# Query and key parts stored once and repeated by the loads, and the values' bias added by VectorE, in a four-layer network on one Trainium2 core

## The chip, the core and the metric

The kernel runs on one core of a Trainium2 chip (trn2). The core has TensorE (PE in the profile, with PEld for its weight loads), VectorE (DVE), ScalarE (ACT), GpSimd (POOL), SyncE (SP, which here only issues DMA transfers), and 16 DMA engines that move data between HBM and the on-chip memories. The metric is the device time of one execution in microseconds, the median over runs. Lower is better.

## The reference

A residual network of four layers on `x` of shape 8 x 512 x 128. Every layer adds an attention and a feed-forward of the same normalised input. The three attentions that the change touches, with 16 heads of 8 numbers each:

```python
# layer 0: causal, with alibi                     (8 batches, 512 tokens)
qkv = x @ w_qkv.T + b_qkv;  q, k, v = heads(qkv)
scores = q @ k.T / sqrt(8) - (distance), masked;  out = softmax(scores) @ v
return out @ w_out.T + b_out
# layer 2: causal, relative positions
scores = (Q @ K.T + Q @ pek[idx].T) / sqrt(8), masked;  attn = softmax(scores)
out = attn @ V + attn @ pev[idx];  return out @ Wo.T
# layer 3: no mask; queries, keys and values are one projection
q = x @ wq.T + bq;  out = softmax(q @ q.T / sqrt(128)) @ q;  return out @ wu.T + bu
```

Layer 1 is a linear attention, which the change leaves alone. The feed-forwards are two blockwise fp4 layers, a local attention network, and a routed mixture of 8 experts.

## The kernel before

The stages run one after the other, each in a `Scope` that ends with a barrier of all engines. Scores are products of bf16 numbers that together keep fp32 accuracy: every query and every key is split into three bf16 parts of 8 rows each (first, second, third), and a product over 48 rows sums six pairings of parts. So the contraction needs the query parts in the order 1,2,3,1,2,1 (`QROWS`) and the key parts in the order 1,1,1,2,2,3 (`KROWS`).

**The projection**, `split_projection` (L725), runs for each attention before it, over 8 batches of 512 tokens. A job is one projection of one batch: TensorE makes `h_ps` (L750), ScalarE writes `FULL` and the first part (L769, L773), VectorE makes the other two parts (L783, L785, L787), and SyncE and GpSimd store the parts to DRAM (`query_rows_d`, `key_rows_d`), six stores of 128 KB per job: part 1 three times, part 2 twice, part 3 once, so that the DRAM copy has all 48 rows. Even ones are issued by SyncE (L797), odd ones by GpSimd (L818); in layer 3, where GpSimd scatters rows for the experts, SyncE issues all 12 of a job. `PARTS` is a ring of four; ScalarE waits for the stores of job i-4 before it writes it again. Layers 0 and 2 have two jobs per batch (queries, keys) and also the values: four 128x128 products of the batch with the weights, each followed by a one-row product that adds the bias (L756, L757), and a copy by ScalarE (L776). The DRAM rows are read only after the projection's barrier.

**The causal and the last attention**, `turned_attention` (L826), is written out step by step for t from -14 to the end, 32 steps per batch. Two groups of heads live in SBUF rows 0 to 47 and 64 to 111 of `QS` and `KS`. SyncE loads two batches ahead (L922, L925): four transfers of 48 rows, 384 KB each, in pieces of 1 KB in layer 0 and 512 B in layer 3 (there keys go to `KN`, and GpSimd regroups them). In the order of SyncE's queue, the loads of batch b+2 come at step 33 of batch b (keys of layer 3 at step 20). Behind them in the same queue stand, for each quad T of heads (8 steps), four small transfers of the row maxima, `a_soft_QS<-a_soft_MT` (L964, L966), two rows each, issued at step 8T-5. TensorE waits for them at step 8T before the turned scores (L1064). At the start come loads of batch 0, four `alibi_d` transfers of 4 rows x 16 pieces of 1 KB in layer 0 (L941), and loads of batch 1.

**The relative attention**, `relative_heads` (L277), goes in quads of four heads, 32 quads. At the start of each quad SyncE issues the loads of the next one (L361): 48 rows of 4 KB for the queries and 48 for the keys, 192 KB each. For each head it then issues the band load, the skew store, two bias loads and two band stores. TensorE first needs the next quad's operands four scores later, in `relative` (L497). SyncE's queue is in order: an instruction that waits holds all behind it.

The profile drops the layer's digit from names: `a_proj_PARTS` is the tile of `a0_proj`, `a2_proj` or `a3_proj`.

## Time and profile before

| | us |
|---|---|
| median of 3 runs (4264.11 to 4271.95) | 4265.2 |
| the profiled execution | 4260.68 |
| its span in the trace | 4258.7 |
| projection of layer 0, first product to last ScalarE copy | 63.7 to 111.6 |
| causal attention, first product | 151.9 |
| projection of layer 2 | 2359.2 to 2416.1 |
| relative attention, first product | 2432.2 |
| projection of layer 3, first product | 3555.3 |
| last attention, first product | 3817.6 |

The rest are the feed-forwards, the linear attention, norms and set-up. The mean granted TensorE clock of the profiled execution was 0.783 of full speed. The profile's page gives totals; what a change in one stage does is read from the timeline of that stage, engine by engine: the start of an instruction, its length, and in brackets how long its engine sat idle before it and what released it.

### The profile page before, as it was taken

What the parts mean: (1) busy time and instruction counts of PE and PEld (TensorE: products, weight loads), DVE (VectorE), ACT (ScalarE), POOL (GpSimd) and SP (SyncE); (2) the same over time, 40 slices, a digit from 0 to 9 for tenths busy, and PEclk for the clock granted to TensorE, in tenths of its full rate; (3) what the DMA queues carried; (4) which work ended last, traced back from release to release, by engine and by line L of the source; (5) the groups of instructions that cost most, each with busy time, mean ns of one, the idle gap of its engine ahead of it and who ended that gap; (6) DMA issues with size and microseconds to landing.
All of it is one profiled execution on the core that took longest, in us unless ns stands there. A gap on an engine that the chain in (4) does not pass through costs nothing. (4 is left out here: it accounts for less than half of the span.)

```text
span 4258.7 us, 67695 instructions
## 1 busy us (share of the span) xinstructions
PE 2931.0 (69%) x21547; PEld 1596.1 (37%) x21547; DVE 2349.2 (55%) x4792; ACT 1746.5 (41%) x4244; POOL 826.7 (19%) x1061
## 2 busy tenths in 40 slices
PE   5588846374635787777776687777778722768885
PEld 2344424253423444444443343333333311762221
DVE  4556467454855566666663354444445453138885
ACT  2355511211213455455553244444444401227775
POOL 2100001021113444444441300000000004112220
PEclk9789867686767999999998666666666655889998
DMA  3432110000001000000000577777777615663331
GB/s 113 79 56 52 38 53 0 8 1 6 1 14 48 10 19 18 18 10 18 18 18 3 170 189 196 187 192 192 187 193 192 161 42 158 174 146 55 66 61 37
DMA packets 462309, 340.77 MB, mean 80 GB/s; under 512 B 64351, under 2 KB 424986, under 8 KB 461986
## 3 DMA queue, kind: packets, MB, share of 16 engines
q1 hardware_dynamic: 441474, 308.78, 29.4%
q0 software_dynamic: 8704, 20.99, 1.8%
q10 hardware_dynamic: 11808, 7.08, 0.6%
q8 instruction: 155, 2.54, 0.3%
q14 instruction: 168, 1.38, 0.1%
HBM read 174.71 MB, written 146.81 MB: 75 GB/s over the span
## 5 line engine op out<-in xcount | busy, mean ns | idle before, releaser
L1158 DVE TENSOR_REDUCE a_soft_NM<-a_soft_s_ps 128x2 f32<-128x1024 f32 (+3 forms) x512 | 514.2, 1021 | 204.3 <-PE a_soft_s_ps L1093 132.8
L1192 ACT ACTIVATE a_soft_PTS<-a_soft_st_ps 128x512 f32<-128x512 f32 (+3 forms) x1024 | 458.3, 521 | 147.9 <-PE a_soft_st_ps L1069 101.7
L465 PE MATMUL a_soft_pt_ps<-net_ident,a_soft_PR 128*128 128x128 f32 x1280 | 330.1, 370 | 123.2 <-ACT a_soft_PTS L567 115.8
L613 ACT ACTIVATE a_soft_PR<-a_soft_s_ps,a_soft_least 128x128 f32<-128x128 f32 (+3 forms) x512 | 263.9, 527 | 338.7 <-DVE a_soft_least L588 241.8
L1064 PE MATMUL a_soft_st_ps<-a_soft_QS,a_soft_KS 50*128 50x512 bf16 (+4 forms) x1024 | 257.8, 359 | 60.1 <-ACT a_soft_PTS L1192 32.2
L465 PEld LDWEIGHTS a_soft_pt_ps<-net_ident,a_soft_PR 128*128 128x128 f32 x1280 | 184.1, 181 | 220.8 <-ACT a_soft_PR L613 160.0
L1106 PE MATMUL a_soft_o_ps<-a_soft_PTS,a_soft_VR 128*32 128x512 f32 (+3 forms) x2048 | 240.9, 544 | 0.1
L2275 PE MATMUL f_run_ps<-f_run_WQKV,f_run_HT 128*128 128x512 f32 x384 | 228.9, 687 | 15.2 <-DVE f_run_RS L1496 8.0
L2608 ACT ACTIVATE f_run_PB<-f_run_ps,f_run_MX 128x128 f32<-128x128 f32 x512 | 180.3, 378 | 134.0 <-DVE f_run_MX L2490 134.0
L2413 POOL TENSOR_TENSOR f_run_QK<-f_run_QK,f_run_T 128x512 f32<-128x512 f32 x128 | 163.4, 1277 | 365.6 <-DVE f_run_T L2468 363.2
L569 DVE COPY a_soft_PTS<-a_soft_pt_ps 128x512 f32<-128x512 f32 (+3 forms) x320 | 169.5, 530 | 72.6 <-PE a_soft_pt_ps L465 40.0
L588 DVE CUSTOM_DVE_ANT_0 a_soft_s_ps<-a_soft_s_ps,a_soft_BIAS 128x128 f32<-128x128 f32 (+1 forms) x256 | 92.9, 363 | 205.1 <-PE a_soft_s_ps L510 177.4
L583 DVE TENSOR_REDUCE a_soft_far_least<-a_soft_s_ps 128x1 f32<-128x128 f32 (+1 forms) x256 | 91.2, 356 | 192.8 <-PE a_soft_s_ps L510 191.5
L510 PE MATMUL a_soft_s_ps<-a_soft_KS,a_soft_QS 48*128 48x128 bf16 (+3 forms) x512 | 194.5, 380 | 1.1 <-ACT a_soft_PR L613 0.9
L2252 PE MATMUL f_run_ps<-net_ident,f_run_PB 128*128 128x128 f32 x512 | 88.2, 330 | 154.5 <-DVE f_run_PB L2478 154.5
L439 POOL COPY a_soft_VR<-net_XN 128x128 f32 (+1 forms) x32 | 9.4, 296 | 918.3 <-PE a_soft_o_ps L486 918.1
L2490 DVE TENSOR_REDUCE f_run_MX<-f_run_ps 128x8 f32<-128x1024 f32 x64 | 78.4, 1225 | 188.3 <-PE f_run_ps L2242 188.3
L567 ACT ACTIVATE a_soft_PTS<-a_soft_pt_ps 128x512 f32<-128x512 f32 (+3 forms) x320 | 149.1, 466 | 74.9 <-PE a_soft_pt_ps L465 67.2
L2421 POOL TENSOR_TENSOR f_run_QK<-f_run_QK,f_run_RN 128x512 f32<-128x512 f32 x128 | 169.0, 1320 | 31.3 <-issue 18.2
L1064 PEld LDWEIGHTS a_soft_st_ps<-a_soft_QS,a_soft_KS 54*128 54x128 bf16 (+1 forms) x1024 | 72.0, 94 | 264.0 <-ACT a_soft_PTS L1192 182.1
L1088 PE MATMUL a_soft_s_ps<-a_soft_QS,a_soft_KS 48*128 48x512 bf16 x512 | 118.4, 397 | 53.3 <-DMA a_soft_QS<-query_rows_d 27.6
L2252 PEld LDWEIGHTS f_run_ps<-net_ident,f_run_PB 128*128 128x128 f32 x512 | 70.8, 166 | 198.3 <-issue 198.3
(382 smaller groups left out, 6395.5 us busy)
## 6 DMA issues: line engine op xcount, KB each, us to landing
a_soft_BIAS<-skew_d SPq DMA_DIRECT2D x256, 191.0 KB, 4.3
band_d<-a_soft_PR SPq DMA_DIRECT2D x256, 191.0 KB, 3.8
skew_d<-a_soft_RS SPq DMA_DIRECT2D x128, 256.0 KB, 4.5
a_soft_PB<-band_d SPq DMA_DIRECT2D x128, 256.0 KB, 3.1
f_run_W<-in_L_ffn_w SPq DMA_DIRECT2D x72, 256.0 KB, 2.7
query_rows_d<-a_proj_PARTS SPq DMA_DIRECT2D x96, 128.0 KB, 3.4
key_rows_d<-a_proj_PARTS SPq DMA_DIRECT2D x96, 128.0 KB, 3.8
a_soft_QS<-query_rows_d SPq DMA_DIRECT2D x32, 384.0 KB
```

The costliest lines, as they stand in the source:

```text
L465: last = pe.transpose(pt_ps[:, slot, kb * P:(kb + 1) * P], PR[:, n % NPR, OFF + kb * P:OFF + (kb + 1) * P], ident[:])
L510: pe.matmul(s_ps[:, n % 4, 0:w], q_blk(sl, h, j), KS[:, sl, h * S:h * S + w], start=True, stop=True).then_inc(scores_ready, 1)
L569: eng.tensor_copy(dst, src).then_inc(pt_copied[0], 1)
L613: act.activation(PR[:, n % NPR, OFF:OFF + width(j)], s_ps[:, n % 4, 0:width(j)], ACT.Exp, bias=least[:, n:n + 1], scale=-1.0).then_inc(pro ...
L1064: last = pe.matmul(st_ps[:, e % 3, q0:S], cols(KS, KX, buf, par, g, kb * P, P), cols(QS, KX, buf, par, g, q0, S - q0), start=True, stop=fu ...
L1106: last = pe.matmul(o_ps[32 * h:32 * h + 32, q0:S], VR[:, T % 2, h, kb, :], PTS[:, T % 2, h, kb, q0:S], start=(kb == 0), stop=(kb == TB - 1 ...
L1158: dve.tensor_reduce(NM[:, T % 2, j, p, :], s_ps[:, ring["s", a] % 2, :, 0:width(j)], AX.X, ALU.max, negate=True).then_inc(max_ready, 1)
L1192: act.activation(PTS[:, T % 2, 2 * p + par, kb, q0:S], st_ps[:, e % 3, q0:S], ACT.Exp, scale=scale).then_inc(probs_ready, 1)
L2275: pe.matmul(out, HT[:, j * P:(j + 1) * P], WQKV[:, v // B, i * LINNER:(i + 1) * LINNER], start=True, stop=True).then_inc(m["q_ready"], 1)
L2413: pool.tensor_tensor(QK[:, j, i, :], QK[:, j, i, :], T2[:, i, :], ALU.add).then_inc(m["added"], 1)
L2421: pool.tensor_tensor(heads(QK[:, j, i, :]), heads(QK[:, j, i, :]), bcast(RN[:, j, i, :], 64), ALU.mult).then_inc(m["qk_scaled"], 1)
L2608: last = act.activation(PB[:, j % 2, h, :], ps[:, where["s", v, j] + h // 4, (h % 4) * P:(h % 4 + 1) * P], ACT.Exp, bias=MX[:, j % 2, h:h ...
```

## The change

- In three attentions the projection stores every part once (`PART_ROWS`): three stores of 128 KB per job, two by SyncE and one by GpSimd; in layer 3 three by SyncE per batch. The DRAM tensors have 24 rows. Layer 3 keeps one tensor, and both its queries and keys are read from it.
- Each load of 48 rows becomes three (`PAIRS`): rows 0 to 23, 24 to 39 and 40 to 47 of the SBUF tile. For queries they read parts 1-3, 1-2 and 1. For keys they read part 1 three times, part 2 twice and part 3 once, by a source whose outermost dimension has step 0 and size 3 or 2. Bytes per load stay the same. `turned_attention` has 12 load transfers per batch for 4, `relative_heads` 6 per quad for 2.
- The values' bias is loaded once into all 128 partitions (`shift`), the one-row products are gone, and VectorE's addition (after the batch's last job) replaces ScalarE's copy.
- The small stages that filled the row of ones are gone.

```diff
-    NDMA = 2
+    NDMA = 6
...
                 for t, src in ((QS, qd3), (KS, kd3)):
-                    sp.dma_start(t[:, sl, :], src[ds(b, 1), :, u * 4 * S:(u + 1) * 4 * S].rearrange("a p f -> (a p) f")).then_inc(opnd_loaded[sl], 16)
+                    for n, (at, m) in enumerate(PAIRS):
+                        of = src[ds(b, 1), :, u * 4 * S:(u + 1) * 4 * S].rearrange("a p f -> (a p) f")
+                        rows = t[at * HD:(at + m) * HD, sl, :]
+                        if src is qd3:
+                            sp.dma_start(rows, of[0:m * HD, :]).then_inc(opnd_loaded[sl], 16)
+                        else:
+                            of = of[n * HD:(n + 1) * HD, :]
+                            sp.dma_start(rows, bass.AP(of.tensor, of.offset, [[0, m]] + [list(d) for d in of.ap])).then_inc(opnd_loaded[sl], 16)
...
-QROWS = ((0, 0), (8, 1), (16, 2), (24, 0), (32, 1), (40, 0))
-KROWS = ((0, 0), (8, 0), (16, 0), (24, 1), (32, 1), (40, 2))
+PART_ROWS = ((0, 0), (8, 1), (16, 2))
+PAIRS = ((0, 3), (3, 2), (5, 1))
...
-                        pe.matmul(out, XNT[:, b * S + j * P:b * S + (j + 1) * P], values[0], start=True, stop=False)
-                        last = pe.matmul(out, values[2], values[1], start=False, stop=True)
+                        last = pe.matmul(v_ps[:, b % 2, j * P:(j + 1) * P], XNT[:, b * S + j * P:b * S + (j + 1) * P], values[0],
+                                         start=True, stop=True)
...
-                if values is not None:
-                    act.wait_ge(v_ready, b + 1)
-                    act.activation(values[3][:, 4 * b:4 * b + 4, :, :].rearrange("p a h (j d) -> p (a h) j d", d=HD),
-                                   v_ps[:, b % 2, :].rearrange("p (j h d) -> p h j d", j=TB, d=HD), ACT.Copy).then_inc(v_copied, 1)
...
+                if values is not None and i % NJ == NJ - 1:
+                    b = i // NJ
+                    dve.wait_ge(v_ready, b + 1)
+                    shift = bass.AP(values[1].tensor, values[1].offset, [list(values[1].ap[0]), [HD, H], [0, TB], [1, HD]])
+                    dve.tensor_tensor(values[2][:, 4 * b:4 * b + 4, :, :].rearrange("p a h (j d) -> p (a h) j d", d=HD),
+                                      v_ps[:, b % 2, :].rearrange("p (j h d) -> p h j d", j=TB, d=HD), shift, ALU.add).then_inc(v_copied, 1)
...
-            def load(b, t, d, sem):
+            def load(b, t, d, queries, sem):
                 for par in range(2):
-                    dst = t[64 * par:64 * par + KR6, b % 2, :]
...
+                    for n, (at, m) in enumerate(PAIRS):
+                        dst = t[64 * par + at * HD:64 * par + (at + m) * HD, b % 2, :]
+                        of = d[b, 0:m * HD] if queries else d[b, n * HD:(n + 1) * HD]
...
+                        if not queries:
+                            of = bass.AP(of.tensor, of.offset, [[0, m]] + [list(x) for x in of.ap])
+                        sp.dma_start(dst, of).then_inc(sem, 16)
```

SyncE's queue in the relative attention at the start of a quad, before: operands of the next quad (L361), band load, skew store, bias loads, band stores.

```order
L361 DMA a_soft_QS<-query_rows_d 48x2048
L361 DMA a_soft_KS<-key_rows_d 48x2048
L394 ISA
L395 DMA a_soft_PB<-band_d 128x4x128
L365 REGISTER_ALU
L368 DMA skew_d<-a_soft_RS 128x4x128
```

The same place in the changed kernel, where the query loads are L365, the key loads L368 and the band load L402.

```order
L365 DMA a_soft_QS<-query_rows_d 24x2048
L365 DMA a_soft_QS<-query_rows_d 16x2048
L365 DMA a_soft_QS<-query_rows_d 8x2048
L368 DMA a_soft_KS<-key_rows_d 24x1x2048
L368 ISA
L368 DMA a_soft_KS<-key_rows_d 16x1x2048
L368 ISA
L368 DMA a_soft_KS<-key_rows_d 8x2048
L398 REGISTER_ALU
L401 ISA
L402 DMA a_soft_PB<-band_d 128x4x128
```

Four more transfers stand ahead of the band load and of all that follows it.

SyncE's queue in the causal attention, the loads of batch b+2 and what is next behind them, before:

```order
L966 DMA a_soft_QS<-a_soft_MT 2x512 x4
L925 DMA a_soft_KS<-key_rows_d 48x8x512 x2
L925 DMA a_soft_QS<-query_rows_d 48x8x512 x2
L980 DMA heads_d<-a_soft_OS 9x512 x4
L966 DMA a_soft_QS<-a_soft_MT 2x512 x4
```

And in the changed kernel the loads of that place alone (now L938):

```order
L938 DMA a_soft_KS<-key_rows_d 24x8x512
L938 DMA a_soft_KS<-key_rows_d 16x8x512
L938 DMA a_soft_KS<-key_rows_d 8x8x512
L938 DMA a_soft_KS<-key_rows_d 24x8x512
L938 DMA a_soft_KS<-key_rows_d 16x8x512
L938 DMA a_soft_KS<-key_rows_d 8x8x512
L938 DMA a_soft_QS<-query_rows_d 24x8x512
L938 DMA a_soft_QS<-query_rows_d 16x8x512
L938 DMA a_soft_QS<-query_rows_d 8x8x512
L938 DMA a_soft_QS<-query_rows_d 24x8x512
L938 DMA a_soft_QS<-query_rows_d 16x8x512
L938 DMA a_soft_QS<-query_rows_d 8x8x512
```

The head stores and the row maxima (now L993 and L979) come eight transfers later in the queue.

VectorE's row in the projection of layers 0 and 2, changed kernel: the addition of the values stands behind every second job.

```order
L785 TENSOR_TENSOR a_proj_REST<-a_proj_FULL,a_proj_PARTS 128x512
L787 CAST a_proj_PARTS<-a_proj_REST 128x512
L789 TENSOR_TENSOR a_proj_PARTS<-a_proj_REST,a_proj_PARTS 128x512
L794 TENSOR_TENSOR a_vall<-a_proj_v_ps,a_shift 128x512
L785 TENSOR_TENSOR a_proj_REST<-a_proj_FULL,a_proj_PARTS 128x512
```

VectorE has seven instructions per batch where it had six, and ScalarE four where it had five.

## Rows read from the trace of the kernel before

**Rows 1.** Page, part 1: each engine's busy time, share of span, instructions.
```profile
PE 2931.0 (69%) x21547; PEld 1596.1 (37%) x21547; DVE 2349.2 (55%) x4792; ACT 1746.5 (41%) x4244; POOL 826.7 (19%) x1061
```

**Rows 2.** Timeline, SyncE queue, causal attention: start us, length, line, transfers.
```profile
203.62 1.33 SPq L925 DMA_DIRECT2D a_soft_KS<-key_rows_d  x2
204.99 1.28 SPq L925 DMA_DIRECT2D a_soft_QS<-query_rows_d  x2
...
210.43 2.54 SPq L966 DMA_DIRECT2D a_soft_QS<-a_soft_MT  x4
217.01 0.62 SPq L987 DMA_DIRECT2D a_soft_SC<-heads_d  x1
```

**Rows 3.** Timeline, TensorE, same place; idle before and releaser in brackets.
```profile
217.60 0.43 PE L1064 MATMUL a_soft_st_ps<-a_soft_QS,a_soft_KS 54*128 54x512 bf16 x2 [3.60 <-DMA a_soft_QS<-a_soft_MT]
```

**Rows 4.** Windows: engines' busy times, TensorE clock, DMA share, GB/s.
```profile
132.00:142.00 10.00, 0.00 (x0) 0.00 (x0) 0.00 (x0) 0.00 (x0) 0.68 (x3) 0.50 1.14 162
154.00:155.00 1.00, 0.73 (x12) 0.40 (x8) 1.00 (x2) 0.00 (x0) 0.00 (x0) 0.50 0.27 87
155.00:156.00 1.00, 0.38 (x7) 0.14 (x4) 1.00 (x2) 0.00 (x0) 0.00 (x0) 0.50 0.33 99
```

**Rows 5.** DMA view, window 153 to 157 us: packets by size.
```profile
DMA packets 276, 0.28 MB, mean 70 GB/s; under 512 B 19, under 2 KB 275, under 8 KB 275
```

**Rows 6.** Timeline, SyncE, start of the causal attention.
```profile
130.47 1.34 SPq L925 DMA_DIRECT2D a_soft_KS<-key_rows_d  x2
...
134.25 0.70 SPq L941 DMA_DIRECT2D a_soft_KS<-alibi_d  x2
```

**Rows 7.** Timeline, TensorE, first product of the causal attention.
```profile
151.89 0.30 PE L1088 MATMUL a_soft_s_ps<-a_soft_KS,a_soft_QS 52*128 52x128 bf16 x2 [40.93 <-DMA a_soft_KS<-alibi_d]
```

**Rows 8.** Timeline, SyncE, relative attention, one group's load.
```profile
2707.76 0.48 SPq L361 DMA_DIRECT2D a_soft_QS<-query_rows_d  x1
2708.34 1.01 SPq L361 DMA_DIRECT2D a_soft_KS<-key_rows_d  x1
2711.24 0.39 SPq L395 DMA_DIRECT2D a_soft_PB<-band_d  x1
```

**Rows 9.** Timeline, TensorE, relative attention, same group.
```profile
2713.18 0.60 PE L497 MATMUL a_soft_r_ps<-a_rel_k,a_soft_QS 48*128 48x128 bf16 x4 [1.66 <-DMA a_soft_KS<-key_rows_d]
```

**Rows 10.** Waits, 2600 to 3200 us: engine, line, releaser, us, times, longest.
```profile
PE a_soft_r_ps L497 <- DMA a_soft_KS<-key_rows_d: 32.9, 15, 3.1
```

**Rows 11.** Timeline, SyncE, last attention, a key load in the loop.
```profile
3869.46 1.33 SPq L922 DMA_DIRECT2D a_soft_KN<-key_rows_d  x2
...
3878.03 2.73 SPq L964 DMA_DIRECT2D a_soft_QS<-a_soft_MT  x4
```

**Rows 12.** Timeline, TensorE, last attention, first product and first turned product.
```profile
3817.60 1.03 PE L1088 MATMUL a_soft_s_ps<-a_soft_QS,a_soft_KS 48*128 48x512 bf16 x4 [27.57 <-DMA a_soft_QS<-query_rows_d]
...
3835.11 0.61 PE L1064 MATMUL a_soft_st_ps<-a_soft_QS,a_soft_KS 50*128 50x512 bf16 x2 [1.21 <-DMA a_soft_QS<-a_soft_MT]
```

**Rows 13.** Tile a_proj_v_ps: ns min/median/max, first and last start.
```profile
L776 ACT ACTIVATE a_vall<-a_proj_v_ps x8: 597/597/601, 70.8 to 111.0; 128x512 f32<-128x512 f32 x8
L776 ACT ACTIVATE net_XN<-a_proj_v_ps x8: 597/597/598, 2368.5 to 2415.5; 128x512 f32<-128x512 f32 x8
```

**Rows 14.** Timeline, TensorE, values of one batch, third projection.
```profile
2381.36 0.48 PE L757 MATMUL a_proj_v_ps<-a_rows 1*128 1x128 f32 x2
2381.77 1.99 PE L750 MATMUL a_proj_h_ps<-net_XNT,a_W 128*128 128x512 f32 x2
```

**Rows 15.** Timeline, VectorE, same projection, one job to the next.
```profile
2384.92 0.69 DVE L783 TENSOR_TENSOR a_proj_REST<-a_proj_FULL,a_proj_PARTS 128x512 f32<-128x512 f32 x1 [2.83 <-ACT a_proj_PARTS L773]
...
2386.79 0.69 DVE L783 TENSOR_TENSOR a_proj_REST<-a_proj_FULL,a_proj_PARTS 128x512 f32<-128x512 f32 x1
```

**Rows 16.** Timeline, SyncE, end of the causal attention's projection.
```profile
113.43 2.94 SPq L797 DMA_DIRECT2D key_rows_d<-a_proj_PARTS  x3
```

**Rows 17.** Timeline, TensorE, first product after the last layer's projection.
```profile
3647.46 1.12 PE L2050 MATMUL f_run_xt_ps<-net_ident,f_run_ROWS 128*128 128x128 f32 x4 [82.36 <-DMA f_run_ROWS<-expert_rows_d]
```

66 lines of the change are left out of this document (29 added, 37 removed).

## The prediction

> **What bounds the kernel now.** I read the page first: TensorE is busy 2931.0 us, 69% of the span [rows 1], so no engine is full over the whole, and each of the three attentions must be read in its own timeline. In the causal attention I followed SyncE through one load of the operands. Four transfers are issued from 203.62 to 206.3, the row maxima (`MT`) of the next quad from 210.43 to 213.0 [rows 2], and TensorE then sits idle for 3.60 us until 217.60, released by those maxima [rows 3]. The store of the heads' results issued in between is as late: SyncE's next instruction, which waits for it, starts at 217.01 [rows 2]. So what is queued behind a load lands behind it, and a load here lies on the path already. At the start, TensorE's first product waits until 151.89 for the alibi rows [rows 7], which are issued at 134.25 behind the loads of batch 0 [rows 6]. In the relative attention the loads are issued at 2707.76 and 2708.34 [rows 8], TensorE waits for them 1.66 us until 2713.18 [rows 9], and it does so in 15 of some 20 quads, 32.9 us in 600 [rows 10]. In the last attention the first product waits for operands until 3817.60 and the first turned product for maxima until 3835.11 [rows 12]. The projections of layers 0 and 2 take 5.74 and 6.71 us per batch (7 periods from 70.8 to 111.0 and from 2368.5 to 2415.5) [rows 13], and there TensorE goes from one batch to the next without a gap. The projection of layer 3 ends when GpSimd has scattered the experts' rows: TensorE waits 82.36 us [rows 17].
>
> **How a transfer is spread, and what a piece costs.** This decides the case. While all 16 DMA engines work on loads into 48 rows, they move 162 GB/s (132 to 142 us), 10.1 GB/s or 101 ns per KB each. From 154 to 156 us the share falls to 0.27 and 0.33, that is 4 to 5 of 16 engines, with 87 and 99 GB/s [rows 4]. The stretch 153 to 157 has 276 packets, 19 of them small [rows 5], so 257 of 1 KB: the 4 x 64 pieces of the four alibi transfers, whose outermost dimension is 4. They were spread over four engines though each had 64 pieces to share, and these four engines end later than the rest by exactly that work. Alone, they moved about 22 GB/s each, 47 ns per KB. I conclude that an engine's share is cut from the outermost dimension. The new key loads have an outermost source dimension of 3 and 2 (24 and 16 rows in SBUF), and a common cut of both sides gives 3 and 2 engines; the query loads are cut in 12, 16 and 8. No row shows such a repeated source, and if the cut follows the SBUF rows it would be 12 and 16 engines; both are kept. The Trainium skill, "DMA: Bandwidth & Descriptors", section "Why a DMA increments its semaphore by 16 and not by 1", says that a transfer runs on the largest number of engines up to 16 that divides the slowest dimensions of both sides, lowest-numbered first, and its rules for kernel authors warn of a leading zero-stride broadcast. The alibi rows agree. By it the sum is the one below; without it, rival A.
>
> The first engine's work for one batch of `turned_attention` is then, for each of the two head groups, keys 64 + 64 + 8 KB and queries 16 + 8 + 8 KB, together 336 KB against 96 KB before. The row maxima, two rows, use the same first engines.
>
> **Causal attention, six loads in the loop.** Before: 96 KB at 101 ns, 10 us, seen as 205.3 to 215.3, and maxima 2.3 us later. After: 336 KB at 47 ns is 15.8 us; the queries' part (64 KB) is shared with many engines and may go at 60 to 100 ns, so 17 to 19 us, and I take 17.5. SyncE's eight more issues at 0.65 us each (1.33 for two [rows 2]) end before that and cost nothing. The next maxima land 7.5 us later, and nothing covers it, since TensorE waits for them now: 6 x 7.5 = 45 us. Bounds per load: 5 us (47 ns throughout) and 25 us (101 ns throughout: 34 us for 10). **Its start:** loads of batch 0 end 7.5 us later, but alibi pieces behind them, now contended, go faster: +3.5; the first maxima wait for batch 1's load: +4.5. Together 8 (3 to 42).
>
> **Relative attention, 31 loads.** The first engine has 84 KB per quad (21 pieces of 4 KB) for 24. At 47 ns per KB it is 3.9 us against 2.4 at the contended rate: +1.5. Four more issues at 0.5 us each, from the rows' 0.48 and 1.01 [rows 8], put the last key transfers 2 us later, partly beside that: together +3, between +1 (issue and data overlap) and +8 (84 KB at 101 ns plus issue). SyncE then waited until 2711.24 for the band's stores, so it is not itself held up. TensorE waits already, and its next loads are tied to the same quad's end, so the delay recurs: 31 x 3 = 93 us (31 to 250).
>
> **Last attention.** Keys alone are 272 KB on the first engine, in 512 B pieces. At 47 to 54 ns per KB that is 13 to 14.7 us against 4.9. Start: keys +9, then the queries, so the first product +9; first maxima behind batch 1's load, +4. In the loop keys are issued at 3869.46 and the maxima at 3878.03 [rows 11]; keys end at 3871.3 + 14 = 3885.3, the maxima about 2.3 later at 3887.6, where 3880.8 + 2.3 = 3883.1 was enough: +4 each, x 6 = 24. The query loads (128 KB for 96) end before their maxima are issued: 0. Together 37 (15 to 145).
>
> **Gains.** One-row products: a pair starts at 2381.36 and the next product at 2381.77 [rows 14], 0.41 us, four per batch, 1.66 us. VectorE's two jobs take 2 x 1.87 (2384.92 to 2386.79 [rows 15]) and the addition, of the size of its 0.69 us subtraction, 0.7: 4.45 us. Layer 2: 6.71 becomes 5.05, TensorE still last, 8 x 1.66 = 13. Layer 0: 5.74 - 1.66 is 4.1, so VectorE's 4.45 is last in the fast half: 8 to 12, I take 10. ScalarE loses a copy that nothing waited for. Stores: layer 0's last six are issued until 116.37, the last three taking 2.94 us [rows 16], and four of a batch's instead of six on SyncE end some 2 us sooner, in both layers 1.5 to 2. A stage less in layer 2, 1. Layer 3: the scatter is last anyway, 0, unless its wait of 82 us were the stores'. Sum -28 (-20 to -34).
>
> **The sum.** The profiled execution took 4260.7 us, 4.5 under the median of the three. 4260.7 + 8 + 45 + 93 + 37 - 28 = 4415.7. I take 4415.
>
> **Rivals.** A: the cut follows the SBUF rows, so all or 12 engines share. The first engine's rows are 8 for 6 in a relative quad and 128 KB for 96 in a batch of the others: +3 us x 6, +5 at the starts, and in the relative attention issue alone, +1 to +2 x 31; 18 + 5 + 46 - 28 = +41, 4302. For it: no row has a repeated source. Against it: the alibi transfers. B, the side of faster: the loads land no later than now, because a repeated row comes cheaper and the issue overlaps; then only the gains stay, 4233. The point is 0.9 us more per relative quad (28 / 31). For it: the loads of the relative attention run beside other traffic; against it: TensorE waits for them in three of four quads. C: few engines are no faster than many on these rows, 101 ns per KB: 6 x 25 + 42 + 250 + 145 - 28 = +559, 4820. Against it: rows 4, on four engines. Between forecast and C lies a part of it, as where a longer wait also lowers the granted TensorE clock in the relative attention.
>
> **How the numbers follow.** Forecast 0.69, A 0.14, B 0.08, C 0.09. A measurement of this kernel tells 0.2%, 8.5 us, from no change. Faster is B with 0.08, within 0.2% is the low edge of A, 0.03, slower the rest, 0.89. The forecast's own range is 4330 to 4540 (low and middle bounds); to hold 8 in 10 it reaches into A and a little towards C: 4290 to 4570.
>
> **What would show it.** In the profile after: at each load of the causal attention TensorE idles about 11 us on `MT` (3.60 now) with a DMA share near 0.2; the wait of L497's successor is 4 to 5 us per quad; the key loads' landings grow most; projections run at 5.05 and about 4.5 to 5 us per batch. If the DMA share stays at one in the loads, the step on spreading is wrong and A holds; if it falls but landings take 35 us, C.

## The result, and the profile after

The changed kernel takes 4440.0 us (median, 4433.5 to 4446.9), the kernel before 4268.6 beside it: a ratio of 1.039, 95% interval 1.0375 to 1.0405. It is slower by 171 us; 4415 was forecast, with 4290 to 4570 as the range. The profiled executions, 4433.53 and 4260.68 us, differ by 172.9.

The spans of the two traces, cut at the same events, give this account. The right column is what the same stage was forecast to add.

| stage | before, us | after, us | difference | forecast |
|---|---|---|---|---|
| set-up, to the first product of layer 0's projection | 63.6 | 65.5 | +1.9 | 0 |
| projection of layer 0 with its drain | 56.9 | 42.2 | -14.7 | -12 |
| causal attention, start | 44.8 | 56.9 | +12.1 | +8 |
| causal attention, first to last turned product | 358.6 | 424.1 | +65.5 | +45 |
| middle layers and the set-up of layer 2 | 1835.3 | 1850.8 | +15.5 | -1 |
| projection of layer 2, to the first relative product | 73.0 | 51.0 | -22.0 | -15 |
| relative attention, first to last product | 970.7 | 1030.6 | +59.9 | +93 |
| to the first product of the last attention | 414.7 | 422.9 | +8.2 | +9 |
| last attention, to the first turned product | 17.5 | 22.0 | +4.4 | +4 |
| last attention, turned products | 382.2 | 423.5 | +41.3 | +24 |
| the end | 41.4 | 42.2 | +0.8 | 0 |

The sum is near and the large signs are as forecast, but three terms are off by 17 to 33 us, and the middle, where -1 was forecast, lost 15.5.

SyncE's queue in the causal attention of the changed kernel (timeline: start us, length, line, transfers), where [rows 2] stood:

```profile
199.90 2.43 SPq L979 DMA_DIRECT2D a_soft_QS<-a_soft_MT  x4
202.71 10.54 SPq L938 DMA_DIRECT2D a_soft_KS<-key_rows_d  x6
213.30 6.15 SPq L938 DMA_DIRECT2D a_soft_QS<-query_rows_d  x6
219.50 1.53 SPq L993 DMA_DIRECT2D heads_d<-a_soft_OS  x4
221.07 2.52 SPq L979 DMA_DIRECT2D a_soft_QS<-a_soft_MT  x4
```

And TensorE at that place (timeline; in brackets the idle time before and its releaser), for [rows 3]:

```profile
228.02 0.62 PE L1077 MATMUL a_soft_st_ps<-a_soft_QS,a_soft_KS 54*128 54x512 bf16 x2 [14.93 <-DMA a_soft_QS<-a_soft_MT]
```

Read the two together. The wait on the maxima grew from 3.60 to 14.93 us. The maxima are issued at 221.07, 21.2 us after the previous ones, where it was 9.6 (200.81 to 210.43). From their issue to TensorE's product it is 6.95 us now and was 7.17. By the semaphore events of both traces, maxima of a quad without a load land 3.4 to 3.6 us after their issue, and those behind a load 5.8 to 7.4. So the maxima wait behind the load on the DMA engines in both kernels alike, some 3 us, and what has grown is that they are issued late. SyncE spends 16.7 us in issuing twelve transfers.

The six transfers of the keys take 1.76 us each as a mean, where one of 48 rows took 0.67, but they are not alike. Here are the first (24 rows, outermost dimension 3) and the last (8 rows, outermost dimension 8):

```profile
202.71 0.80 SPq L938 DMA_DIRECT2D a_soft_KS<-key_rows_d  x1
209.91 3.34 SPq L938 DMA_DIRECT2D a_soft_KS<-key_rows_d  x1
```

The second took 0.70 and the fifth 3.28. So it is not its own shape that makes an issue long, but what has been issued in front of it. The kernel before shows the same where loads pile up: at the start of its causal attention the last of eight operand loads, of 48 rows, is held too.

```profile
141.52 3.07 SPq L925 DMA_DIRECT2D a_soft_QS<-query_rows_d  x1
```

While SyncE issues the keys the DMA engines are far from busy (windows: TensorE, its weight loads, VectorE, ScalarE, GpSimd, granted clock, DMA share, GB/s):

```profile
204.00:209.00 5.00, 4.54 (x68) 2.50 (x66) 3.57 (x6) 4.18 (x10) 0.29 (x1) 1.00 0.22 54
209.00:214.00 5.00, 3.95 (x64) 2.07 (x60) 3.30 (x4) 2.52 (x9) 0.00 (x0) 1.00 0.18 61
...
222.00:226.00 4.00, 0.00 (x0) 0.00 (x0) 0.00 (x0) 0.00 (x0) 0.00 (x0) 0.50 0.13 42
```

A share of 0.18 to 0.22 is three to four engines of sixteen while the keys are issued; [rows 4] had 1.14 in such a load. In between, with the queries, it rises to 0.73. At the end it is two engines at 20 GB/s each.

In the relative attention TensorE waits for the operands 71.0 us in 18 quads of a stretch of 600 us (waits, 2690 to 3290 us: engine, line, releaser, us, times, longest), where [rows 10] had 32.9 in 15:

```profile
PE a_soft_r_ps L504 <- DMA a_soft_KS<-key_rows_d: 71.0, 18, 6.3
```

One such quad, SyncE and then TensorE, for [rows 8] and [rows 9]:

```profile
2784.09 2.44 SPq L365 DMA_DIRECT2D a_soft_QS<-query_rows_d  x3
2786.62 2.26 SPq L368 DMA_DIRECT2D a_soft_KS<-key_rows_d  x3
2789.12 0.41 SPq L402 DMA_DIRECT2D a_soft_PB<-band_d  x1
```

```profile
2792.74 0.60 PE L504 MATMUL a_soft_r_ps<-a_rel_k,a_soft_QS 48*128 48x128 bf16 x4 [3.96 <-DMA a_soft_KS<-key_rows_d]
```

In the last attention a key load in the loop, for [rows 11], is held at the issue too: 12.88 us for six transfers, so the maxima follow 17.9 us after the previous ones instead of 11.6.

```profile
3997.35 2.64 SPq L977 DMA_DIRECT2D a_soft_QS<-a_soft_MT  x4
4000.04 12.88 SPq L938 DMA_DIRECT2D a_soft_KN<-query_rows_d  x6
4012.96 2.27 SPq L990 DMA_DIRECT2D heads_d<-a_soft_OS  x4
4015.27 2.70 SPq L977 DMA_DIRECT2D a_soft_QS<-a_soft_MT  x4
```

The term that was not seen stands in the set-up of layer 2. SyncE's queue there in the changed kernel:

```profile
2394.73 1.45 SPq L137 DMA_DIRECT2D a_shift<-in_L_attn_pev  x1
2396.23 10.33 SPq L137 DMA_DIRECT2D a_far_key<-in_L_attn_pek  x16
2420.04 0.35 SPq L255 DMA_DIRECT2D a_turn_ring<-in_L_attn_Wq  x1
```

and in the kernel before:

```profile
2331.00 0.58 SPq L137 DMA_DIRECT2D a_rows<-in_L_attn_pev  x1
2331.63 5.54 SPq L137 DMA_DIRECT2D a_far_key<-in_L_attn_pek  x16
2339.57 0.35 SPq L255 DMA_DIRECT2D a_turn_ring<-in_L_attn_Wq  x1
```

From the bias load to the next stage it is 25.3 us, and was 8.6. The windows of the changed kernel show nothing at work in it but DMA at 4 GB/s:

```profile
2396.00:2406.00 10.00, 0.00 (x0) 0.00 (x0) 0.00 (x0) 0.00 (x0) 0.00 (x0) 0.50 0.05 4
2406.00:2416.00 10.00, 0.00 (x0) 0.00 (x0) 0.00 (x0) 0.00 (x0) 0.00 (x0) 0.50 0.07 4
```

The projections gained more than forecast. VectorE's addition in the two of them (ns min/median/max, first and last start), for [rows 13]:

```profile
L794 DVE TENSOR_TENSOR a_vall<-a_proj_v_ps,a_shift x8: 682/684/686, 72.7 to 103.0; 128x512 f32<-128x512 f32 x8
L794 DVE TENSOR_TENSOR net_XN<-a_proj_v_ps,a_shift x8: 682/684/686, 2446.5 to 2477.1; 128x512 f32<-128x512 f32 x8
```

Seven periods are 4.33 us each in layer 0 and 4.37 in layer 2. What TensorE does meanwhile in layer 2 is in the windows of the kernel before,

```profile
2380.00:2390.00 10.00, 10.00 (x32) 5.56 (x31) 5.48 (x10) 3.56 (x7) 5.69 (x11) 0.77 0.74 220
2390.00:2400.00 10.00, 10.00 (x30) 5.35 (x28) 5.19 (x9) 5.22 (x9) 3.78 (x8) 0.72 0.86 261
```

and of the changed one:

```profile
2450.00:2456.00 6.00, 4.87 (x21) 2.60 (x20) 5.63 (x10) 3.23 (x6) 1.39 (x4) 1.00 0.62 182
2456.00:2462.00 6.00, 4.39 (x22) 2.85 (x23) 5.56 (x11) 3.21 (x6) 1.39 (x3) 1.00 0.64 188
```

Before, TensorE was busy without a gap at a granted clock of 0.72 to 0.77. Now it is busy 73 to 81% of the time at 1.00, the level of 2.4 GHz, and VectorE is busy 93 to 94%. The projection of layer 2 that was TensorE's is VectorE's. In layer 0 the clock was not always low before: from 90 to 110 us TensorE was busy without a gap at 1.00.

```profile
90.00:110.00 20.00, 20.00 (x80) 12.35 (x80) 12.77 (x22) 12.10 (x20) 11.68 (x23) 1.00 0.90 275
```

So these windows show which clock each projection had, and not what sets it.

### The profile page after: what moved, and what is told of

The parts are those of the page before. It is cut to its first block and busy times, and to the rows that moved or that the text cites. A ratio compares the mean times of both kernels' runs of the same rounds, so it can differ in the third digit from the quotient of the medians.

```text
span 4431.7 us, 67657 instructions
## 1 busy us (share of the span) xinstructions
PE 2883.7 (65%) x21419; PEld 1559.6 (35%) x21419; DVE 2359.1 (53%) x4806; ACT 1738.0 (39%) x4228; POOL 791.3 (18%) x997
## 3 DMA queue, kind: packets, MB, share of 16 engines
q1 hardware_dynamic: 429760, 295.28, 26.3%
## 5 line engine op out<-in xcount | busy, mean ns | idle before, releaser
L2434 POOL TENSOR_TENSOR f_run_QK<-f_run_QK,f_run_RN 128x512 f32<-128x512 f32 x128 | 168.9, 1319 | 31.3 <-issue 17.9
L504 PE MATMUL a_soft_r_ps<-a_rel_k,a_soft_QS 48*128 48x128 bf16 x512 | 65.1, 264 | 147.4 <-DMA a_soft_KS<-key_rows_d 124.9
```

The lines of the kernel that those rows point to most:

```text
L2434: pool.tensor_tensor(heads(QK[:, j, i, :]), heads(QK[:, j, i, :]), bcast(RN[:, j, i, :], 64), ALU.mult).then_inc(m["qk_scaled"], 1)
```

## The experiments

The profiled run of each is cut at the same events. They ran in four groups, each on one chip: `e1` to `e4`, `e5` to `e8`, `e9` to `e11`, and `e12`. In the second and third group the kernel before takes 4318 and 4317 us instead of 4269 to 4271, so a kernel is compared by its ratio to the kernel before on the same chip. The edits of `e4`, `e9`, `e10` and `e11` also load the small table of relative keys in three transfers for six; the set-up of layer 2 shows nothing of it beyond the noise. For the stages in the second group I take those of `e8_fewer_stores`, which is the kernel before outside layer 2: causal loop 360.0 us, relative attention 965.5, last attention from its first product to its last turned one 436.0. In the third group `e9_once_layer2` is the kernel before in the two turned attentions: causal loop 356.9 us. The noise shows in stages that no edit touches: the relative attention took 974.0 and 977.8 us in `e1` and `e2`, against 970.7 in the kernel before. So 7 us there are no result. The projection of layer 0 varies too where no edit touches it: from its first product to the first load of the attention it took 66.8 us in the kernel before, and 73.8, 66.9, 65.4 and 71.3 in `e3`, `e5`, `e7` and `e8`.

One stage depends on the chip by much more. After the projection of layer 3, TensorE waits 82.36 us in the kernel before [rows 17], and 102.73 in `e9_once_layer2`, which has the same twelve stores per batch there; `e5`, `e6`, `e7`, `e8` and `e11` wait 102.6 to 104.2. With three or six stores per batch the wait is 82 us in all four kernels that have them, also in `e10_once_all` (six), which ran on the chip of `e9_once_layer2`:

```profile
3645.76 0.47 PE L2057 MATMUL f_run_xt_ps<-net_ident,f_run_ROWS 128*128 128x128 f32 x1 [102.73 <-DMA f_run_ROWS<-expert_rows_d]
3647.69 0.69 PE L2060 MATMUL f_run_xt_ps<-net_ident,f_run_ROWS 128*128 128x128 f32 x2 [82.27 <-DMA f_run_ROWS<-expert_rows_d]
```

In `e9_once_layer2` the six stores of a batch's keys take SyncE up to 9.07 us to issue there, 3.8 to 4.1 in the kernel before. So on the chips of the second and third group the fewer stores of layer 3 save 20 us that they do not save on the first.

**Where the gains and the unseen loss are.** First, the values' bias alone, stores and loads of the parts as before:

```diff
-                        pe.matmul(out, XNT[:, b * S + j * P:b * S + (j + 1) * P], values[0], start=True, stop=False)
-                        last = pe.matmul(out, values[2], values[1], start=False, stop=True)
+                        last = pe.matmul(v_ps[:, b % 2, j * P:(j + 1) * P], XNT[:, b * S + j * P:b * S + (j + 1) * P], values[0],
+                                         start=True, stop=True)
...
+                    dve.tensor_tensor(values[2][:, 4 * b:4 * b + 4, :, :].rearrange("p a h (j d) -> p (a h) j d", d=HD),
+                                      v_ps[:, b % 2, :].rearrange("p (j h d) -> p h j d", j=TB, d=HD), shift, ALU.add).then_inc(v_copied, 1)
```

> The kernel before with only the values' bias changed: added by VectorE from a 128x128 tile; stores and loads of the operand parts as before. Theory: the gains of the changed kernel's two projections (about 14.6 us in layer 0 and 22 us in layer 2 by its trace) come from the removed one-row products and the lighter TensorE, and stay here; the new load of the values' bias in layer 2 costs 16.6 us, and the set-up of layer 0 1.8 us. So 4268.6 - 14.6 - 22 + 16.6 + 1.8 = 4250 us. Rival: the gains came from the fewer stores (3 transfers for 6 of each job). Then a batch still takes 5.7 and 6.7 us here, the load's cost is left, and the time is about 4285 us.

Measured: 4267.9 us, ratio 0.9997 (0.9986 to 1.0008). Middle and set-up of layer 2 +15.7, as in the changed kernel. The projection of layer 2 takes 63.3 us against 73.0 before and 51.0 in the changed kernel, layer 0 is about 4.5 us better up to the first causal product. The time lies between the two that were given, and both accounts were half right: the removed products give 9.7 of the 22 us. ScalarE shows what holds the rest (groups of instructions, projection of layer 2: busy, mean ns, idle before and its releaser):

```profile
L772 ACT ACTIVATE a_proj_PARTS<-a_proj_h_ps,a_far_key 128x512 bf16<-128x512 f32 x8 | 5.5, 688 | 9.7 <-DMA key_rows_d<-a_proj_PARTS 9.7
L772 ACT ACTIVATE a_proj_PARTS<-a_proj_h_ps 128x512 bf16<-128x512 f32 x8 | 4.8, 595 | 9.1 <-DMA query_rows_d<-a_proj_PARTS 9.1
```

It waits for the stores to leave the ring of `PARTS`. In the changed kernel these waits are gone.

The same with a bias of 8 numbers per partition:

```diff
-shift = s.sb("shift", [P, P])
+shift = s.sb("shift", [P, HD])
...
-(shift[:].rearrange("p (h d) -> p h d", d=HD), bass.AP(pev.tensor, pev.offset, [[0, P], [0, H], [1, HD]]))
+(shift[:], bass.AP(pev.tensor, pev.offset, [[0, P], [1, HD]]))
```

> The same as e1_bias_only, but in layer 2 the bias is loaded as 8 elements per partition (128 pieces instead of 2048 of 32 B) and repeated over the heads by the operand's zero step when VectorE adds it. Theory: the 16.6 us that the set-up of layer 2 gained in the changed kernel are those 2048 pieces of 32 B out of one place; then this kernel takes 15 to 16 us less than e1_bias_only, about 4235 us. Rival: the set-up is late for another reason (the sixteen far_key transfers, of which one batch took 10.33 instead of 5.54 us to issue, wait for something else); then it takes the same time as e1_bias_only.

Measured: 4250.3 us, ratio 0.9953 (0.9934 to 0.9972), 17.6 below `e1_bias_only`. SyncE's queue in the set-up of layer 2:

```profile
2326.81 0.43 SPq L137 DMA_DIRECT2D a_shift<-in_L_attn_pev  x1
2327.29 5.39 SPq L137 DMA_DIRECT2D a_far_key<-in_L_attn_pek  x16
2335.04 0.35 SPq L255 DMA_DIRECT2D a_turn_ring<-in_L_attn_Wq  x1
```

8.2 us from the bias load to the next stage. The 2048 pieces of 32 B were the unseen loss, and this kernel beats the one before by 0.5%. Whether it is their number or that all read the same 32 B is not separated: the small load still reads one place, 128 times.

Then the stores alone, in layer 2, products as before. This kernel leaves out half of the rows that the loads then read, so its scores in layer 2 are not the reference's; its times can still be compared:

```diff
-    None, -float(1 / np.sqrt(HD)), ((qd, QROWS),)) ... far_key[:, 0:1], 1.0, ((kd, KROWS),))
+    None, -float(1 / np.sqrt(HD)), ((qd, QROWS[0:3]),)) ... far_key[:, 0:1], 1.0, ((kd, KROWS[0:3]),))
```

> The kernel before, but in layer 2 only the first three of the six row sets of queries and keys are stored; the loads are as before and read old rows for the others, so layer 2's scores are not the reference's. Theory: of the 22 us that the projection of layer 2 gained in the changed kernel, about 11 are the halved stores (e1_bias_only, without them, gained 9.7): this kernel's projection of layer 2 takes 11 us less than before, 4259 us. Rival: the stores gain something only where the one-row products are gone, because TensorE is last with them; then it takes the time of before, 4270 us.

Measured: ratio 1.0005 (0.9988 to 1.0022), the projection of layer 2 at 69.4 us, where a kernel with that projection unchanged took 73.6 on the same chip (`e7_even_cut`). So the stores alone give about 4, the products alone 10, both together 22: each hid the other. The total cannot show 4 us in 4317. TensorE's products of the jobs took a mean of 1045 ns there, 666 in the changed kernel.

**Number of transfers or their engines.** The loads cut in three without a repeated source:

```diff
-                    sp.dma_start(t[:, sl, :], src[ds(b, 1), :, u * 4 * S:(u + 1) * 4 * S].rearrange("a p f -> (a p) f")).then_inc(opnd_loaded[sl], 16)
+                    of = src[ds(b, 1), :, u * 4 * S:(u + 1) * 4 * S].rearrange("a p f -> (a p) f")
+                    for at, m in PAIRS:
+                        sp.dma_start(t[at * HD:(at + m) * HD, sl, :], of[at * HD:(at + m) * HD, :]).then_inc(opnd_loaded[sl], 16)
```

> The kernel before, stores of 48 rows and the one-row products as before, but every load of queries and keys cut into three transfers of 24, 16 and 8 rows, none with a repeated source. It has the changed kernel's number of load transfers. Theory (few engines): the delay of the changed kernel comes from sources repeated along their outermost dimension; here the transfers go over many engines and only the issues and an uneven cut are left, 1 to 3 us per load in the causal and last attention and 1 to 1.5 per quad in the relative one: 4268.6 + 12 to 36 + 31 to 46, about 4330 us (4310 to 4350). Rival (issues): SyncE's twelve issues for four set the delay, whatever the engines; then the causal loop loses 10.8 us per load, the relative attention 1.9 per quad and the last attention 56 in all, as in the changed kernel: 4268.6 + 65 + 12 + 60 + 56, about 4460 us.

Measured: 4311.8 us, ratio 1.010 (1.0084 to 1.0117). Causal loop +21.7 (3.6 per load), relative attention +4.8, which is within the noise, last attention +6.9 and +4.2 at its start. The first causal product comes 10.6 us later, but 7 of them are the projection of layer 0, which the edit does not touch; from the first load's issue to the first product it is 25.2 us for 21.4. The few-engines account holds, and the relative attention does not mind six issues for two.

The changed kernel with its repeated sources spread (relative attention: rows in the order element, copy; turned attentions: six transfers of 8 rows):

```diff
-                            sp.dma_start(rows, bass.AP(of.tensor, of.offset, [[0, m]] + [list(d) for d in of.ap])).then_inc(opnd_loaded[sl], 16)
+                        sp.dma_start(rows, bass.AP(of.tensor, of.offset, [[row, HD], [HD * row if src is qd3 else 0, m]] + rest)).then_inc(opnd_loaded[sl], 16)
```

> The changed kernel with the repeated source spread. In the relative attention the rows of a group of 24, 16 or 8 lie in the order element, then copy, so that the outermost dimension of every source is 8 (six transfers per quad, as in the changed kernel). In the causal and last attention the keys come as six transfers of 8 rows for each head group instead of three, so a load has 18 transfers where the changed kernel has 12, and none repeats its source. Theory (few engines): relative attention loses 1 us or less per quad for 1.9, causal loop 4 to 6 us per load for 10.8, last attention 25 for 56, in spite of the six more issues: 4440 - 30 - 35 - 30, about 4345 us (4320 to 4380). Rival (issues): the relative attention stays as in the changed kernel, the two others grow by half: 4440 + 32 + 28, about 4500 us.

Measured: 4343.9 us, ratio 1.0169 (1.0152 to 1.0186), 96 below the changed kernel although a turned load has 18 transfers instead of 12. Relative attention +26.3 for +59.9, causal loop +44.7 for +65.5 (7.4 per load), last attention +21.7 for +45.8. TensorE's wait for the operands in the relative attention (waits, whole stage, `e4_rows_spread` and then the changed kernel):

```profile
PE a_soft_r_ps L502 <- DMA a_soft_KS<-key_rows_d: 85.0, 27, 4.6
```

```profile
PE a_soft_r_ps L504 <- DMA a_soft_KS<-key_rows_d: 124.9, 30, 6.3
```

Before it was 58.4 and in `e3_split_only` 62.7. The key rows are still read again here, and their outermost dimension is 8; which of the two costs the 26.3 is not separated.

A repeated source differs from a plain one in two ways: its outermost dimension is short, and the same rows are read again. To part them, six sets of rows were stored as before, but the keys' nine rows apart, so that three sets cannot be merged into 24 rows:

```diff
-KROWS = ((0, 0), (8, 0), (16, 0), (24, 1), (32, 1), (40, 2))
+KROWS = ((0, 0), (9, 0), (18, 0), (27, 1), (36, 1), (45, 2))
...
+                            part = bass.AP(of.tensor, of[9 * at:9 * at + 1, :].offset, [[9 * H * S, m], [H * S, HD], [1, 4 * S]])
```

> As e3_split_only (six copies of each row set stored, loads of 24, 16 and 8 rows, no source read twice), but the copies of the keys lie nine rows apart in DRAM instead of eight, so the sources of the keys' 24 and 16 rows keep an outermost dimension of 3 and 2, as the repeated ones of the changed kernel have. Theory (outermost dimension): the loops lose what they lose in the changed kernel, 9 to 11 us per load in the causal attention (e3_split_only 3.6), 1.5 to 2 per quad in the relative one (e3_split_only 0.15), 45 in the last attention from its first product (e3_split_only 7), so about 4311.8 + 43 + 52 + 39 = 4446 us (4420 to 4460). Rival (the same rows read again): it is reading one DRAM row three times that is slow, then the time is e3_split_only's, 4312 us.

Measured: 4504.1 us, ratio 1.0429 (1.0397 to 1.046), against 1.010 of `e3_split_only`. Causal loop +68.7 (11.4 per load), relative attention +60.6, last attention +36 where the changed kernel lost 45.8: nearly the changed kernel's losses, with no row read twice. In 5 us of its key loads (216 to 221 us) the DMA share is 0.19, three engines, where `e3_split_only` has 0.42 (214 to 219 us). It is the outermost dimension, not the rereading. The rule in the Trainium skill, "DMA: Bandwidth & Descriptors", section "Rules for kernel authors", that an outermost dimension of size c holds a transfer to at most c engines, agrees with these runs.

What is left in `e3_split_only` could be the number of issues or the uneven cut (24, 16 and 8 rows give the first engines four rows instead of three):

```diff
-PAIRS = ((0, 3), (3, 2), (5, 1))
+PAIRS = ((0, 2), (2, 2), (4, 2))
```

> As e3_split_only, but the loads are cut in three transfers of 16 rows instead of 24, 16 and 8. The number of issues is the same; the first engines' share is 3 rows again as in the kernel before instead of 4. Theory (share of the first engines): the 21.7 us that e3_split_only lost in the causal loop fall to 5 or less and the 7 in the last attention to 2, about 4285 us. Rival (issues): twelve issues for four cost the 3.6 us per load by themselves; then the time is e3_split_only's, 4312 us.

Measured: ratio 1.0042 (1.0026 to 1.0058). Causal loop +12.1, last attention +2.2, relative attention none; from the first load's issue to the first causal product 24.1 us for 21.9. Neither account is right alone: of 3.6 us per load in the causal loop some 1.6 are the uneven cut and 2.0 the eight more issues. `e3_split_only` ran on another chip, so this split is rough.

**What holds the maxima.** The traces of all these kernels can be put side by side at the same load of the causal attention. The third column is the time between two issues of maxima around the load, less the 9.6 us of the kernel before; the last is the loop's loss divided by six.

| kernel | SyncE's time for the keys' transfers | maxima issued later by | loss per load |
|---|---|---|---|
| changed | 10.54 (6) | 11.6 | 10.9 |
| e5_gap | 9.14 (6) | 11.0 | 11.4 |
| e4_rows_spread | 8.76 (12) | 8.4 | 7.4 |
| e3_split_only | 4.46 (6) | 3.7 | 3.6 |
| e10_once_all (below) | 4.45 (6) | 4.1 | 4.0 |
| e7_even_cut | 3.88 (6) | 2.6 | 2.0 |

The loss follows the delay of the issue, within 1.1 us. Two rows of `e5_gap` and `e3_split_only` (timeline, SyncE), the same bytes and the same number of transfers, with an outermost dimension of 3 and 2 and without:

```profile
215.21 9.14 SPq L938 DMA_DIRECT2D a_soft_KS<-key_rows_d  x6
```

```profile
214.63 4.46 SPq L930 DMA_DIRECT2D a_soft_KS<-key_rows_d  x6
```

So SyncE is held at its issues behind transfers that few engines carry, and that is how the few engines reach TensorE. What limit holds it (how much may be outstanding, and where) no run shows. Whether the engines themselves delay the maxima as well was asked with the changed kernel and the keys of the loop issued by GpSimd:

```diff
+                if b is not None and b + 2 < B and not full:
+                    pool.wait_ge(st_ready, 64 * (b + 1))
+                    loads[0](b + 2, KN, kd3, False, k_more[b % 2], pool)
```

> The changed kernel, but in the causal attention's loop the keys' six transfers with their repeated sources are issued by GpSimd, on its own queue, instead of by SyncE; everything else as in the changed kernel. Theory (the issue is what holds): in the traces so far the maxima land 6 to 8 us after their issue in every kernel, and the loss per load equals the delay of that issue behind SyncE's twelve transfers (210.43 us in the kernel before, 221.07 in the changed one, two quads alike). Here SyncE issues six and is free after about 6 us, as the kernel before needed it, so the loop's 10.8 us per load fall to 0 to 4, the wait for the maxima from 92 us to 25 to 50, and the ratio to before from 1.039 to 1.024 to 1.029. Rival (the engines are what holds): the key pieces occupy the first two or three engines, the maxima's two rows wait behind them there whoever issues them; then TensorE waits for the maxima as long as in the changed kernel, 80 to 100 us, and the ratio stays at 1.035 to 1.04.

Measured: 4425.2 us, ratio 1.0366 (1.034 to 1.0393), which is the rival's range, and neither range of the wait was met. The causal loop loses 33.6 us instead of 65.5, 5.6 per load, and the wait is (waits, 150 to 640 us, this kernel and then the changed one):

```profile
PE a_soft_st_ps L1083 <- DMA a_soft_QS<-a_soft_MT: 53.9, 8, 9.3
```

```profile
PE a_soft_st_ps L1077 <- DMA a_soft_QS<-a_soft_MT: 92.4, 8, 14.9
```

SyncE's queue and TensorE's product at one load of it:

```profile
254.90 3.33 SPq L941 DMA_DIRECT2D a_soft_QS<-query_rows_d  x4
258.27 2.38 SPq L996 DMA_DIRECT2D heads_d<-a_soft_OS  x4
260.69 2.54 SPq L982 DMA_DIRECT2D a_soft_QS<-a_soft_MT  x4
```

```profile
270.38 0.62 PE L1083 MATMUL a_soft_st_ps<-a_soft_QS,a_soft_KS 54*128 54x512 bf16 x2 [6.69 <-DMA a_soft_QS<-a_soft_MT]
```

Issued in time, the maxima now need 9.7 us to TensorE's product instead of 7. Over the six loads they are issued 10.6 us after the previous ones as a mean (9.6 before) and land 7.9 to 11.9 us after their issue (5.8 to 7.1 before). So both accounts hold a half: with the issue out of the way about half the loss is gone, and the other half is now waiting on the engines. One thing more changed with the edit: the keys moved to a queue of their own. From 170 to 560 us the trace has these packets (DMA queue: packets, MB, share of 16 engines), where the changed kernel has none on q0 (the keys of six loads are 4.7 MB):

```profile
q0 software_dynamic: 7104, 4.81, 9.1%
```

So the half that is left was measured with the keys in another queue than the maxima, and how long the maxima would wait behind them in SyncE's own is not shown. The Trainium skill ("DMA: Bandwidth & Descriptors", "Rules for kernel authors") says of spreading transfers over several issuing engines that it saves issue time only. This case agrees: the loop gained 32 us by it and kept 34. The total gained only 10 to 15 us (by the ratios and by the medians), since the relative attention took 13 us more than in the changed kernel (1043.7 against 1030.6) and the last 4 more, with the same code in both. The 13 us are outside the noise seen elsewhere, and they stay open.

**A better version.** Two more edits on `e2_bias_small`: in layer 2 the queries alone stored once, and in the causal attention the alibi rows ahead of the loads.

```diff
+                for at, m in ((0, 3), (3, 2), (5, 1)):
+                    sp.dma_start(QS[at * HD:(at + m) * HD, sl, :], of[0:m * HD, :]).then_inc(opnd_loaded[sl], 16)
```

> e2_bias_small with two more edits. In layer 2 the queries alone are stored once (three transfers for six) and loaded as 24, 16 and 8 rows out of the 24 stored ones, without a repeated source; and in the causal attention the four alibi transfers, whose outermost dimension is 4, are issued ahead of the loads of batch 0 instead of behind them. Theory: the projection of layer 2 gives 5 us, the relative attention takes back 0 to 5, and the first product of the causal attention comes 3 to 5 us earlier, since the few engines of the alibi rows work while the others wait: 4250.3 - 5 - 3, about 4243 us (4238 to 4250). Rival: the alibi rows ahead delay the loads by as much as they gain, and the split loads cost in the relative attention what the stores save: 4250 us.

Measured: ratio 0.9939 (0.9923 to 0.9956), not to be told from `e2_bias_small`. The projection of layer 2 took 53.4 us for 62.1, more than expected.

The six pairings of parts need no repeated source at all. With the queries' parts in DRAM in the order 3, 2, 1 and the keys' in the order 1, 2, 3, the pairs (3,1) (2,2) (1,3), then (2,1) (1,2), then (1,1) are contiguous blocks on both sides:

```diff
+Q3 = ((0, 2), (8, 1), (16, 0))
+K3 = ((0, 0), (8, 1), (16, 2))
...
+                    for at, m in PAIRS:
+                        r0 = (3 - m) * HD if src is qd3 else 0
+                        sp.dma_start(t[at * HD:(at + m) * HD, sl, :], of[r0:r0 + m * HD, :]).then_inc(opnd_loaded[sl], 16)
```

In layer 2 alone:

> e2_bias_small, and in layer 2 the parts are stored once and loaded in three transfers of 24, 16 and 8 rows, with no repeated source: the queries' parts lie in DRAM in the order 2, 1, 0 and the keys' in the order 0, 1, 2, so the six pairs (2,0) (1,1) (0,2), (1,0) (0,1) and (0,0) are contiguous blocks of both. The turned attentions are as before. Theory: the projection of layer 2 gets the changed kernel's 22 us less than before (11 more than e2_bias_small), the relative attention loses 0 to 5 us as in e3_split_only: 0.9953 of before less 0.0026 to 0.0014, ratio about 0.993 (0.9915 to 0.9945). Rival: the split loads of the relative attention take back what the stores save, ratio 0.995 to 0.996.

Measured: ratio 0.9908 (0.9883 to 0.9933), the lowest of all, though its interval meets those of `e6_best` and `e11_alibi_first`. The projection of layer 2 takes 51.0 us, as in the changed kernel, and TensorE's wait for the operands in the relative attention is 66.1 us against 58.4 before.

In all three attentions:

> The same in all three attentions: parts stored once, loaded as contiguous blocks of 24, 16 and 8 rows, 12 transfers per load of the causal and last attention as in the changed kernel, and the small bias. It is the changed kernel without the repeated outermost dimension. Theory (outermost dimension): what is left of the changed kernel's loss is e3_split_only's 22 us in the causal loop and 7 in the last attention, with 3 to 4 at its start; the projections give 36 us against before, less the start of the causal attention (5 to 10 us, the alibi rows behind twelve issues): ratio to before 0.998 to 1.003, about 4270 us on a chip where before takes 4268. Rival (issues and stores): it stays near the changed kernel without its bias load, ratio 1.03 or more.

Measured: ratio 0.9956 (0.9942 to 0.9971), where the changed kernel had 1.039. It has the same 24 rows in DRAM, the same number of loads and, but for layer 3 (six stores per batch for three, since queries and keys differ in their order), of stores, and no source with a repeated dimension. It also has the small bias, which is 16 us of the difference. And the ratio is lower than the 0.998 to 1.003 expected because of the chip: the fewer stores of layer 3 save 20 us, 0.5%, on this one and nothing on the changed kernel's. Taken off, that gives some 1.000, an estimate. Causal loop +24 us (381.1 against 356.9), relative wait 63.7 us. One load of its causal attention, SyncE and TensorE:

```profile
195.05 4.45 SPq L935 DMA_DIRECT2D a_soft_KS<-key_rows_d  x6
199.54 4.75 SPq L935 DMA_DIRECT2D a_soft_QS<-query_rows_d  x6
...
205.93 2.49 SPq L976 DMA_DIRECT2D a_soft_QS<-a_soft_MT  x4
```

```profile
212.15 0.61 PE L1074 MATMUL a_soft_st_ps<-a_soft_QS,a_soft_KS 54*128 54x512 bf16 x2 [6.72 <-DMA a_soft_QS<-a_soft_MT]
```

Its median is 19 us behind that of `e9_once_layer2`, and its profiled execution 8 us. In the traces the causal loop loses 24 us by its twelve issues and uneven cut, the relative attention 5 and the start of the last one 4; an earlier first product (143.3 for 149.9 us) gives 7 back and the wait in layer 3 another 20. On a chip without that wait it would be further behind.

Last, `e9_once_layer2` with the alibi transfers ahead of the loads of batch 0:

```diff
-            load_keys(0)
-            load_queries(0)
...
+            load_keys(0)
+            load_queries(0)
             load_keys(1)
             load_queries(1)
```

> e9_once_layer2 with the four alibi transfers of the causal attention issued ahead of the loads of batch 0. Theory: their outermost dimension of 4 holds them to four engines, which end last when they come last; issued first they run beside the loads, and the first product comes 3 to 6 us earlier than in e9_once_layer2. Rival: the loads are delayed by as much, the first product comes at the same time within 1 us.

Measured: ratio 0.9933 (0.9908 to 0.9959), 11 us above `e9_once_layer2` in the medians, with the intervals of the ratios meeting; the first causal product at 149.4 us instead of 149.9. The rival holds: moved ahead, the alibi rows gain half a microsecond, and the product, which the alibi rows released before, is now released by the queries.

## Why the prediction was right, and which steps were not

- **How a transfer is spread.** Right, and the main step: [rows 4] and [rows 5] showed four engines for an outermost dimension of four, and `e5_gap` shows the same of 3 and 2 (share 0.19, losses as in the changed kernel). Rival A (the cut follows the SBUF rows) fell; without its gains it gave 4330, and `e3_split_only`, whose loads are cut that way, took 4311.8.
- **Causal attention, loop, 45 us.** Measured 65.5. The step that failed is the sentence that SyncE's eight more issues end before the data and cost nothing. They end at 219.5 and the maxima stand behind them. Two of the keys' six took 3.3 us each where 0.65 was taken for every one: SyncE is held behind the transfers already issued. The prediction has the few engines right and the way to TensorE wrong. Its way (data on the first engine, the maxima behind them there) was worth 3 us in both kernels; with the issue out of the way, in `e12_keys_by_gpsimd`, the loop lost 5.6 us per load. That this is near the 5 to 7.5 that was worked out says little, since the keys were in another queue there.
- **Causal attention, start, 8 us.** Measured 12: 5.3 from the first load's issue to the first product (3.5 forecast) and 6.9 to the first maxima (4.5).
- **Relative attention, 31 x 3 = 93 us.** Measured 59.9, 1.9 per quad. The mechanism was right, the size not: 1.5 us of data and 1.5 of issue were added, and `e3_split_only` (+4.8 in 31 loads) shows that here the four more issues cost 0 to 0.2. What is left, 1.7 to 1.9, comes with the few engines.
- **Last attention, 37 us.** Measured 54 in the table: 8.2 to the first product, 4.4 to the first maxima, as forecast; loop 41 for 24. From the first load's issue to the first product it was 11.5 longer (25.0 for 13.6), 9 forecast; the layer before it happened to be 3 shorter. The loop was mis-sized again because the keys' issue takes 12.88 us and the maxima come 6.3 us later where 4 was taken.
- **Gains, -28 us (27 in the projections).** Measured -36.7. The step that failed took 1.66 us per batch off TensorE's time and left its clock as it was, so that TensorE stayed last at 5.05 us in layer 2. Its clock rose to 1.00, and VectorE's work became the period, 4.37 us there and 4.33 in layer 0, for the 4.45 that was worked out. The saved stores were put at 1.5 to 2 us and gave more, but only together with the saved products.
- **The set-up of layer 2, put at -1.** Measured +15.5, to which the set-up of layer 0 adds 1.9. The load of the values' bias, an edit in the diff, was not costed at all. This was the plain miss of the forecast; the diff shows its 2048 pieces of 32 B.
- The errors in the terms (+4, +20.5, -33, +17, -9, +17) add up to 17 us where their sizes add up to 100. The closeness of the total is in good part luck.
- The low edge of the forecast's own range, 4330, does not follow from its own lower bounds: 3, 30, 31 and 15 less 28 give 4312.
- **Rivals B and C.** B fell with the loads that land later. C (few engines as slow as many) fell too: 6 x 10.9 and 31 x 1.9 are far from 6 x 25 and 31 x 8.

## What to carry to other kernels

Before a copy is moved from a store to a repeated load, look at the outermost dimension that the load then has: a repetition of three or two there left three to four engines of sixteen busy here, and reordering the rows or choosing pairings that are contiguous on both sides keeps the saving without it. Ask of every transfer in an in-order queue how long the queue is held behind it, not only how long its data take, and what stands behind it. A kernel's ratio on one chip can contain a wait that another chip does not have: compare the stages too. Cost each line of a diff, above all the small ones: here a bias tile cost 16 us, more than the 14 us that the rest of the bias edit brought by itself.

## What the runs showed that was not expected

- The issue of a transfer from SyncE's queue is not a fixed cost, and not one of the transfer alone. In the causal loop it is 0.60 to 0.84 us where nothing holds it, for one with an outermost dimension of 3 too (0.80), and 3.28 and 3.34 us for the fifth and sixth of the keys. As a mean of six that is 1.5 to 1.8 us, and 2.1 in the last attention with 512 B pieces (12.88 us for six).
- 2048 pieces of 32 B read from one place of 32 B into 128 partitions take some 16 to 17 us longer than 128 of them, and the loads behind them wait.
- In layer 2 a projection in which TensorE was busy without a gap ran at a granted clock of 0.72 to 0.77; with 73 to 81% busy it ran at 1.00. In layer 0 it was busy without a gap at 1.00. In layer 2 its products of 512 columns went from a mean of 1049 to 666 ns, more than the ratio of the clocks; the rest is not explained.
- Two savings of 4 and 10 us gave 22 together, because ScalarE's wait for stores and TensorE's products each held the same loop.
- Twelve stores per batch beside GpSimd's scatter in layer 3 were free on one chip (a wait of 82 us with them and without) and cost 20 us on two others (103 for 82).
